# Second attention of a fused two-layer kernel: the reciprocal of a chunk's totals cut in two, its second piece and the scaling of z placed behind maxima of the next group

## The chip, the cores and the metric

The kernel runs on one core of one Trainium2 chip. The metric is the device time of one execution in microseconds (us). The kernel before was run three times: 1402.68, 1404.8 and 1405.77 us, median 1404.8 us. One more execution was taken with the hardware profiler: 1403.8 us, with a span of 1401.9 us from the first instruction to the last.

The engines are named as in the profile: PE (TensorE), PEld (its weight loads), DVE (VectorE), ACT (ScalarE), POOL (GpSimd), SP (SyncE, here only the queue that issues the transfers).

## What is computed

Two layers; each computes x + attention(norm(x)) * silu(ffn(norm(x))). The change is in the attention of the second layer, which is an ordinary causal softmax attention over 2048 tokens with 16 heads of 64, written in the reference for one batch row as

```
q = einsum('bsm,hmd->bshd', x, W_Q) + b_Q        # k and v alike
scores = einsum('bqhd,bkhd->bhqk', q, k) / sqrt(64)
scores = where(causal, scores, -inf)
pattern = softmax(scores, axis=-1)
z = einsum('bhqk,bkhd->bqhd', pattern, v)
attn_out = einsum('bqhd,hdm->bqm', z, W_O) + b_O
```

The softmax is done unnormalized: exp(scores - row maximum), its sum over keys (the totals), and z divided by the totals at the end.

## The kernel before, in words

The second attention (`attention1`) fills the last 850 us of the span. It works on pairs of heads (8 pairs, hp), on chunks of 512 queries (4 per pair, qc) and, in a chunk, on tiles of 128 keys (4, 8, 12 and 16 of them, because of the causal mask). One such key tile is a step s. Four steps make a group k; there are 80 groups, ten to a pair. A chunk ends with group 0, 2, 5 or 9 of its pair; the list `ENDS` holds these group numbers.

All orders are fixed by hand. PE goes through a list of units; each unit writes one of three pairs of PSUM banks in turn (the ring, `RING = 3`), and may do so only when the unit three places earlier has been read by its consumer (`room_for`). The units are:

- "scores": eight matmuls of a step (L1800 three products of split queries and keys, L1803 the subtraction of the row maxima). Consumer: ACT, the exponential into `prob` (L1907).
- "maximum": an unsplit product of queries and keys (L1743, with a mask product L1748 on the diagonal) made only for the row maxima of a later chunk. Consumer: DVE, a maximum over the columns (L1964); after the last one of a row tile's block, a small one over the parts (L1972, neg_max).
- "project", "value", "turn", "mix": projections, values, the turning of the maxima, and z times W_O (L1781), which DVE adds to the output (L2037).

A group has a rows phase, in which maxima and the four scores take turns (`rows_phase`; the table `PLACES` says how many maxima stand ahead of each score, so that five maxima give the order maximum, scores, maximum, scores, ... , maximum), then a whole phase with the other units, and then four times "weigh" (L1822), exp times v of the group's four steps into a bank of its own. If the group before ended a chunk, PE puts "total" (L1769) ahead of the weighing: the sum of the chunk's exponentials, which POOL has added up in `acc` (L1706 the first two steps, L1710 one instruction for each further step; L1678 hides the later keys in diagonal tiles). PE writes the totals into one bank, `side_bank`; DVE takes their reciprocal into `inv` (L1985, 512 columns) and multiplies z by it (L1988, in `scale`), both in one go behind the whole phase. The mix of this chunk waits for the scaled z; it stands one or two groups later.

DVE goes through the same list of units in the same order. Its queue is strict: what is issued behind the reciprocal waits for it, and a ring buffer whose maximum DVE has not read yet holds back the third unit after it on PE.

The reciprocal thus stands at five kinds of places, called here by letter. A: last chunk of the pair before, ahead of a rows phase with five maxima (7 times). B: first chunk, ahead of a rows phase with two maxima, one ahead of the first scores and one ahead of the third (8 times; in the first pair there are six maxima). C: second chunk, five maxima (8 times; eight maxima in the first pair). D: third chunk, five maxima (7 times). E: the third chunk of the last pair, ahead of a rows phase without maxima (once). The last chunk of all has lines of its own (L2020, L2021), which stay.

Of the kernel before, what the change touches and what calls it, by code (L numbers as in the profile page):

```python
# [15 lines left out]
P = 128  # L16
# [3 lines left out]
C = 512  # L20
# [1488 lines left out]
def attention1(nc, a, sh, out):  # L1509

    with ExitStack() as ctx:
        def sb(name, shape, dt=F32):
            return ctx.enter_context(nc.sbuf_tensor(name, shape, dt))

        def sem(name):
            return ctx.enter_context(nc.semaphore(name))
# [14 lines left out]
        ENDS = [s // PER for s in CHUNK_LAST]  # L1531
# [22 lines left out]
        def rows_phase(k):  # L1554

            units = []
            first = TC + sum(MAXIMA[:k])
            for j, count in enumerate(PLACES[MAXIMA[k]]):
                units += TILES[first:first + count]
                first += count  # L1560
                if j < PER:
                    units.append(("scores", k * PER + j, None))
            return units

        def whole_phase(k):

            if k < len(STARTING):
                return STARTING[k]
            return [(kind, k // LAPS + ahead, c) for kind, ahead, c in WHOLE[k % LAPS] if k // LAPS + ahead < NP]
# [29 lines left out]
        inv = sb("inv", [P, C])  # L1599
# [20 lines left out]
        totalled = sem("totalled")  # L1620
        inv_done = sem("inv_done1")
# [8 lines left out]
        side_bank = bank[2 * RING + 1]  # L1630
# [82 lines left out]
        def _(pe):  # L1713
# [44 lines left out]
            def total(g):  # L1758
                if g == FINAL:
                    pe.wait_ge(final_summed, T - 1)  # L1760
                else:
                    pe.wait_ge(summed, CHUNK_LAST[g] + 1)
                if g:

                    pe.wait_ge(inv_done, g)
                else:
                    pe.wait_ge(bias_spread, 1)
                for m in range(2):
                    last = nc.tensor.matmul(side_bank[HALF[m], :], sh.ones[:, 0:W], acc[:, g % 2, m, :],  # L1769
                                            start=True, stop=True)  # L1770
                last.then_inc(totalled, 1)
# [84 lines left out]
            for k in range(GROUPS):  # L1856
# [6 lines left out]
                for s in range(k * PER, (k + 1) * PER):  # L1863
                    weigh(s)
            total(NP * NC - 1)
            for unit in LAST:
                fill(unit)
# [69 lines left out]
        def _(dve):  # L1937
# [9 lines left out]
            def split_low(hp, c):  # L1947
                n = AT["project", hp, c]
                src = unit_both[n % RING]
                at = slice(c * C, (c + 1) * C)  # L1950
                done = nth("project", hp, c) * 2
                dve.wait_ge(act_split, done + 1)
                nc.vector.scalar_tensor_tensor(out=k_lo[hp % 2][:, at], in0=src[:, 0, :], scalar=bias[:, 0, hp:hp + 1],
                                               in1=k_hi[hp % 2][:, at].bitcast(F32), op0=ALU.add, op1=ALU.subtract)
                dve.wait_ge(act_split, done + 2)
                nc.vector.scalar_tensor_tensor(out=q_lo[:, at], in0=src[:, 1, :], scalar=bias[:, 1, hp:hp + 1],
                                               in1=q_hi[:, at].bitcast(F32), op0=ALU.add, op1=ALU.subtract)\
                    .then_inc(unit_freed[n % RING], 1)

            def reduce_tile(hp, i, c):  # L1960
                n = AT["maximum", hp, (i, c)]
                cols = min(C, (i + 1) * P - c * C)
                dve.wait_ge(unit_filled, n + 1)
                nc.vector.tensor_reduce(part_max[:, :, i, c], unit_both[n % RING][:, :, 0:cols], AX_X, ALU.max)\  # L1964
                    .then_inc(unit_freed[n % RING], 1)
                if (i + 1) % TC == 0 and c == i // TC:

                    tiles = [u for u in TILES if u[1] == hp and u[2][0] // TC == c]
                    for r in range(RING):
                        for u in [u for u in tiles if AT[u] % RING == r][-1:]:  # L1970
                            wait_freed(dve, u)
                    nc.vector.tensor_reduce(neg_max[:, c % 2, :, 0:TC], part_max[:, :, c * TC:(c + 1) * TC, 0:c + 1],  # L1972
                                            AX_X, ALU.max, negate=True).then_inc(max_done, 1)

            def spread_maxima(hp, c):
                n = AT["turn", hp, c]
                at = slice(c * C, (c + 1) * C)
                dve.wait_ge(unit_filled, n + 1)
                nc.vector.tensor_tensor(max_rows[:, at].rearrange("r (j c) -> r j c", j=TC),
                                        unit_both[n % RING][:, 0, 0:P].unsqueeze(1).to_broadcast([P, TC, P]),  # L1980
                                        own_tile[:, :, :], ALU.mult).then_inc(unit_freed[n % RING], 1)

            def scale(g):
                dve.wait_ge(totalled, g + 1)
                nc.vector.reciprocal(inv[:, :], side_bank).then_inc(inv_done, 1)  # L1985
                dve.wait_ge(inv_done, g + 1)
                dve.wait_ge(z_copied, g + 1)
                nc.vector.tensor_tensor(z[:, g % 2, :], z[:, g % 2, :], inv[:, :], ALU.mult).then_inc(scaled, 1)  # L1988

            def add_final(s):  # L1990
                kt = s - FINAL_FIRST
                q0 = first_column(NC - 1, kt)
                sums = acc[:, FINAL % 2, :, q0:C]
                if kt == 0:
                    return
                if kt >= (NC - 1) * TC:
                    dve.wait_ge(hidden_later, FINAL * TC + kt - (NC - 1) * TC + 1)
                else:
                    dve.wait_ge(exp_done, s + 1)
                if kt == 1:  # L2000

                    dve.wait_ge(totalled, FINAL - 1)
                    nc.vector.tensor_tensor(sums, prob[:, (s - 1) % PR, :, :], prob[:, s % PR, :, :], ALU.add)\
                        .then_inc(final_summed, 1)
                else:
                    dve.wait_ge(final_summed, kt - 1)
                    nc.vector.tensor_tensor(sums, sums, prob[:, s % PR, :, q0:C], ALU.add).then_inc(final_summed, 1)

            def base_final():
                at = slice(T - TC, T)  # L2010
                dve.wait_ge(unit_freed[AT["mix", NP - 2, NC - 1] % RING], FREED["mix", NP - 2, NC - 1])
                link(nc.vector.tensor_tensor(attn[:, at, :], attn[:, at, :], sh.g[:, at, :], ALU.mult))
                link(nc.vector.tensor_tensor(attn[:, at, :], attn[:, at, :], sh.x[:, at, :], ALU.add))
# [19 lines left out]
            def add_mixed(hp, qc):  # L2033
                n = AT["mix", hp, qc]
                tiles = slice(qc * TC, (qc + 1) * TC)
                dve.wait_ge(unit_filled, n + 1)
                nc.vector.tensor_tensor(attn[:, tiles, :], unit_both[n % RING][:, 0, :].rearrange("p (t d) -> p t d", d=D),  # L2037
                                        attn[:, tiles, :], ALU.add).then_inc(unit_freed[n % RING], 1)
                if hp == NP - 1:

                    wait_freed(dve, ("mix", hp, qc))
                    finish(qc)

            def take(unit):
                kind, hp, what = unit
                if kind == "project":
                    split_low(hp, what)
                elif kind == "maximum":
                    reduce_tile(hp, what[0], what[1])
                elif kind == "turn":  # L2050
                    spread_maxima(hp, what)
                elif kind == "mix":
                    add_mixed(hp, what)
# [9 lines left out]
            nc.vector.tensor_copy(attn[:, :, :], row_o[:, :].unsqueeze(1).to_broadcast([P, T, D])).then_inc(bias_spread, 1)  # L2063
            dve.wait_ge(bias_spread, 1)
            for k in range(GROUPS):
                for unit in rows_phase(k):
                    take(unit)
                for unit in whole_phase(k):
                    take(unit)
                if k - 1 in ENDS:  # L2070
                    scale(ENDS.index(k - 1))
                if k == GROUPS - 1:
                    base_final()
                for s in range(k * PER, (k + 1) * PER):
                    if s >= FINAL_FIRST:
                        add_final(s)
# [98 lines left out]
```

## Time and profile before

| what | value |
|---|---|
| three runs, median | 1404.8 us |
| profiled execution: time, span | 1403.8 us, 1401.9 us |
| PE busy | 1309.4 us (93%) |
| DVE busy | 1012.3 us (72%) |
| ACT busy | 750.4 us (54%) |
| POOL busy | 692.1 us (49%) |
| maxima L1964 on DVE | 320 instructions, 336.8 us |
| reciprocals L1985 on DVE | 31 instructions, 103.9 us |

Busy time is the sum of an engine's instructions. A matmul row of the trace starts when its first product is issued; its end is modelled, so consecutive matmuls overlap in the rows. PEclk is the granted TensorE clock as a share of the full 2.4 GHz.

### The profile page before, as it was taken

How to read it: one execution, taken by the hardware profiler on the slowest of the kernel's cores; microseconds unless marked ns; L12 is line 12 of the kernel's file. 1: busy time of each engine (PE TensorE's matmuls, PEld its weight loads, DVE VectorE, ACT ScalarE, POOL GpSimd, SP SyncE). 2: the span in 40 equal slices, each digit the busy share in tenths (PEclk: the TensorE clock that was granted, in tenths of full speed). 3: DMA queues.
4: the chain of work that ended last, by engine and by line, in shares of the span. 5: the costliest groups of instructions: out<-in, count | busy, mean ns of one | idle time of the engine just before them, and what ended most of it. 6: DMA issues, size and time to landing. Idle time of an engine off the chain costs nothing.

```text
span 1401.9 us, 25496 instructions
## 1 busy us (share of the span) xinstructions
PE 1309.4 (93%) x9902; PEld 672.0 (48%) x9902; DVE 1012.3 (72%) x1497; ACT 750.4 (54%) x1204; POOL 692.1 (49%) x527
## 2 busy tenths in 40 slices
PE   5778999999999987999999999999999999999897
PEld 3653222222222245555555555555555555555554
DVE  7666888888888865766766666766666666766768
ACT  5375777877777774434444344444344344444343
POOL 4401150100101010568777677777677677777671
PEclk9899999999999999999999999999999999999999
DMA  3411410000000000000000000000000000000000
GB/s 107 154 73 57 130 24 1 2 1 2 1 1 1 2 1 1 1 1 1 1 1 1 1 1 1 1 1 1 1 0 1 1 1 1 1 1 1 1 16 16
DMA packets 18165, 21.50 MB, mean 15 GB/s; under 512 B 7784, under 2 KB 15872, under 8 KB 16512
## 3 DMA queue, kind: packets, MB, share of 16 engines
q1 hardware_dynamic: 18048, 19.88, 4.5%
q8 instruction: 81, 1.33, 0.4%
q14 instruction: 36, 0.29, 0.1%
HBM read 14.63 MB, written 5.24 MB: 14 GB/s over the span
## 4 chain that ended last, share of the span: by engine, by line
PE 43%; DVE 11%; ACT 3%; issue 1%; POOL 1%; DVEq 0%; POOLq 0%; ACTq 0%
PE psum L1822 13%; PE psum L1800 12%; DVE part_max L1964 4%; PE psum L1743 4%; DVE inv L1985 4%; PE psum L1803 3%; ACT prob L1907 2%; PE psum L1781 2%; PE psum L1730 2%; PE psum L1769 2%; PE psum L1721 1%; DVE z L1988 1%; PE psum L1723 1%; PE psum L1722 1%; PE psum L1748 1%
## 5 line engine op out<-in xcount | busy, mean ns | idle before, releaser
L1710 POOL TENSOR_TENSOR acc<-acc,prob 128x1024 f32<-128x1024 f32 (+3 forms) x250 | 492.8, 1971 | 87.4 <-ACT prob L1907 57.6
L1907 ACT ACTIVATE prob<-psum 128x1024 f32<-128x1024 f32 (+1 forms) x320 | 283.6, 898 | 352.9 <-PE psum L1803 345.7
L1964 DVE TENSOR_REDUCE part_max<-psum 128x2 f32<-128x1024 f32 (+2 forms) x320 | 336.8, 1064 | 168.8 <-PE psum L1743 84.3
L696 DVE TENSOR_SCALAR w<-psum 128x512 f32<-128x512 f32 x472 | 305.2, 686 | 57.2 <-PE psum L553 43.2
L647 ACT ACTIVATE w<-psum 128x512 f32<-128x512 f32 x552 | 293.7, 600 | 84.5 <-PE psum L553 84.2
L573 PE MATMUL psum<-w,v_cols 128*32 128x512 f32 x2048 | 273.6, 607 | 0.0
L1822 PE MATMUL psum<-prob,v_pair 128*64 128x512 f32 (+3 forms) x1280 | 250.2, 532 | 0.7 <-POOL prob L1678 0.7
L1800 PE MATMUL psum<-q_hi,k_hi 64*128 64x512 f32 (+3 forms) x640 | 138.5, 429 | 31.0 <-DVE part_max L1964 21.2
L1822 PEld LDWEIGHTS psum<-prob,v_pair 128*64 128x64 f32 x1280 | 87.4, 137 | 145.2 <-issue 134.2
L1743 PE MATMUL psum<-k_hi,q_hi 64*128 64x512 f32 (+3 forms) x640 | 131.9, 409 | 6.1 <-DVE part_max L1964 4.5
L1800 PE MATMUL psum<-q_lo,k_hi 64*128 64x512 f32 (+3 forms) x640 | 118.8, 367 | 0.0
L1800 PE MATMUL psum<-q_hi,k_lo 64*128 64x512 f32 (+3 forms) x640 | 118.7, 367 | 0.0
L1803 PE MATMUL psum<-max_rows,ones_r 64*128 64x512 f32 (+3 forms) x640 | 118.6, 366 | 0.0
L1985 DVE RECIPROCAL inv<-psum 128x512 f32<-128x512 f32 x31 | 103.9, 3353 | 16.6 <-PE psum L1769 16.6
L553 PEld LDWEIGHTS psum<-q_rows,k_rows 32*128 32x128 f32 x768 | 40.0, 181 | 153.8 <-ACT w L647 146.3
L397 POOL TENSOR_SCALAR xa<-xa,rstd_j,shift_j 128x128 f32<-128x128 f32 x16 | 7.0, 453 | 208.1 <-DVE shift_j L389 208.1
L1678 POOL TENSOR_SCALAR_AFFINE_SELECT prob<-prob 128x256 f32<-128x256 f32 x128 | 53.5, 425 | 110.9 <-ACT prob L1907 109.9
L553 PE MATMUL psum<-q_rows,k_rows 32*128 32x512 f32 x768 | 101.2, 493 | 0.1
L1800 PEld LDWEIGHTS psum<-q_hi,k_hi 64*128 64x128 f32 x640 | 61.0, 187 | 78.9 <-DVE part_max L1964 48.3
L1743 PEld LDWEIGHTS psum<-k_hi,q_hi 64*128 64x128 f32 x640 | 60.9, 186 | 77.1 <-issue 40.8
L1706 POOL TENSOR_TENSOR acc<-prob 128x1024 f32<-128x1024 f32 x23 | 54.8, 2384 | 42.3 <-ACT prob L1907 40.5
L573 PEld LDWEIGHTS psum<-w,v_cols 128*32 128x32 f32 x2048 | 40.6, 108 | 63.6 <-ACT w L647 53.3
(303 smaller groups left out, 1404.7 us busy)
## 6 DMA issues: line engine op xcount, KB each, us to landing
q_rows<-q_dram SPq DMA_DIRECT2D x12, 256.0 KB
k_rows<-k_dram SPq DMA_DIRECT2D x3, 1024.0 KB
q_dram<-parts SPq DMA_DIRECT2D x2, 1024.0 KB, 4.1
k_dram<-parts SPq DMA_DIRECT2D x2, 1024.0 KB, 6.7
x<-in_L_attn_x SPq DMA_DIRECT2D x4, 256.0 KB, 4.0
mask<-in_L_ffn_attention_mask SPq DMA_DIRECT2D x1, 1024.0 KB, 6.1
x_high<-q_dram SPq DMA_DIRECT2D x4, 256.0 KB
x_low<-k_dram SPq DMA_DIRECT2D x1, 1024.0 KB
```

What stands on the lines that cost most here:

```text
L553: last = nc.tensor.matmul(pair_bank[n % RING][i], k_rows[group][rows, kt * P:(kt + 1) * P], q_rows[group][rows, qc * C:(qc + 1) * C], star ...
L573: last = nc.tensor.matmul(out_bank[turn % 2][h * VW:(h + 1) * VW, :], v_cols[group][:, kt, h, :], w[:, s % WR, h, :], start=(kt == 0), sto ...
L647: nc.scalar.activation(w[:, s % WR, 2 * m + i, :], pair_bank[n % RING][i], ACT.Relu)\
L696: nc.vector.tensor_scalar(w[:, s % WR, 2 * m + 1, :], pair_bank[n % RING][1], 0.0, None, ALU.max)\
L1710: nc.gpsimd.tensor_tensor(sums, sums, prob[:, s % PR, :, q0:C], ALU.add).then_inc(summed, 1)
L1743: last = nc.tensor.matmul(to[:, m, 0:n], q_hi[HALF[m], i * P:(i + 1) * P], k_hi[hp % 2][HALF[m], c * C:c * C + n], start=True, stop=not di ...
L1800: nc.tensor.matmul(to[:, m, q0:C], left[HALF[m], keys], right[HALF[m], at], start=n == 0, stop=False)
L1803: last = nc.tensor.matmul(to[:, m, q0:C], ones_r[HALF[m], :], max_rows[HALF[m], at], start=False, stop=True)
L1822: last = nc.tensor.matmul(out_bank[HALF[m], q0:C], v_pair[hp % 2][:, kt, HALF[m]], prob[:, s % PR, m, q0:C], start=kt == 0, stop=kt == (qc ...
L1907: nc.scalar.activation(prob[:, s % PR, :, q0:C], unit_both[n % RING][:, :, q0:C], ACT.Exp, scale=SCALE)\
L1964: nc.vector.tensor_reduce(part_max[:, :, i, c], unit_both[n % RING][:, :, 0:cols], AX_X, ALU.max)\
L1985: nc.vector.reciprocal(inv[:, :], side_bank).then_inc(inv_done, 1)
```

## The change

The reciprocal is issued as two instructions on columns 0 to 383 and 384 to 511. The first piece stands where the whole one stood. The second piece stands behind the first maximum of the next group's rows phase, and the multiplication of z behind its second maximum; where the rows phase has no maxima, both stand behind it. The semaphore `inv_done` now counts two pieces a chunk, and PE's wait ahead of the next total is doubled with it. PE's, ACT's and POOL's programs keep their order, instruction by instruction.

```
-                    pe.wait_ge(inv_done, g)
+                    pe.wait_ge(inv_done, 2 * g)
...
+            def invert(g, part):
+                at = slice(0, C - P) if part == 0 else slice(C - P, C)
+                if part == 0:
+                    dve.wait_ge(totalled, g + 1)
+                nc.vector.reciprocal(inv[:, at], side_bank[:, at]).then_inc(inv_done, 1)
+
             def scale(g):
-                dve.wait_ge(totalled, g + 1)
-                nc.vector.reciprocal(inv[:, :], side_bank).then_inc(inv_done, 1)
-                dve.wait_ge(inv_done, g + 1)
+                dve.wait_ge(inv_done, 2 * (g + 1))
                 dve.wait_ge(z_copied, g + 1)
                 nc.vector.tensor_tensor(z[:, g % 2, :], z[:, g % 2, :], inv[:, :], ALU.mult).then_inc(scaled, 1)
+
+            def end_scale(g, left):
+                if left == 2:
+                    invert(g, 1)
+                else:
+                    scale(g)
+
+            def take_rows(k):
+                g = ENDS.index(k - 2) if k - 2 in ENDS else None
+                left = 2 if g is not None else 0
+                for unit in rows_phase(k):
+                    take(unit)
+                    if unit[0] == "maximum" and left:
+                        end_scale(g, left)
+                        left -= 1
+                while left:
+                    end_scale(g, left)
+                    left -= 1
...
             for k in range(GROUPS):
-                for unit in rows_phase(k):
-                    take(unit)
+                take_rows(k)
                 for unit in whole_phase(k):
                     take(unit)
                 if k - 1 in ENDS:
-                    scale(ENDS.index(k - 1))
+                    invert(ENDS.index(k - 1), 0)
```

DVE at place A, before: the reciprocal, z, and then the five maxima (L1964; part_max) of the next group, with the small maximum over the parts (L1972) behind the first.

```order
L1964 TENSOR_REDUCE part_max<-psum 128x2 x3
L1985 RECIPROCAL inv<-psum 128x512
L1988 TENSOR_TENSOR z<-z,inv 128x512
L1964 TENSOR_REDUCE part_max<-psum 128x2
L1972 TENSOR_REDUCE neg_max<-part_max 128x2x4
L1964 TENSOR_REDUCE part_max<-psum 128x2 x4
L2037 TENSOR_TENSOR xa<-psum,xa 128x4x128
```

The same place after the change (the lines below the edit have moved in the file: L1987 is the reciprocal, L1992 the scaling).

```order
L1987 RECIPROCAL inv<-psum 128x384
L1964 TENSOR_REDUCE part_max<-psum 128x2
L1972 TENSOR_REDUCE neg_max<-part_max 128x2x4
L1987 RECIPROCAL inv<-psum 128x128
L1964 TENSOR_REDUCE part_max<-psum 128x2
L1992 TENSOR_TENSOR z<-z,inv 128x512
L1964 TENSOR_REDUCE part_max<-psum 128x2 x3
L2060 TENSOR_TENSOR xa<-psum,xa 128x4x128
```

The second piece now stands ahead of the second maximum and z ahead of the third.

DVE at place B, which follows: two maxima, and then the addition of the mix (L2037 before, L2060 after), whose product on PE reads the scaled z of this very chunk. First before, then after.

```order
L1985 RECIPROCAL inv<-psum 128x512
L1988 TENSOR_TENSOR z<-z,inv 128x512
L1964 TENSOR_REDUCE part_max<-psum 128x2 x2
L2037 TENSOR_TENSOR xa<-psum,xa 128x4x128
L1979 TENSOR_TENSOR max_rows<-psum,own_tile 128x512
```

```order
L1987 RECIPROCAL inv<-psum 128x384
L1964 TENSOR_REDUCE part_max<-psum 128x2
L1987 RECIPROCAL inv<-psum 128x128
L1964 TENSOR_REDUCE part_max<-psum 128x2
L1992 TENSOR_TENSOR z<-z,inv 128x512
L2060 TENSOR_TENSOR xa<-psum,xa 128x4x128
L1979 TENSOR_TENSOR max_rows<-psum,own_tile 128x512
```

Between z and the mix that needs it there were two maxima; now there is nothing.

## Rows read from the trace of the kernel before

**Rows 1.** Waits of PE: us in total, times, longest.
```profile
PE psum L1800 <- DVE part_max L1964: 21.2, 25, 1.9
```

**Rows 2.** The scaling by its line (ns min/median/max); the 256-column reciprocals by form.
```profile
L1988 DVE TENSOR_TENSOR z<-z,inv x31: 691/693/1392, 579.4 to 1368.9; 128x512 f32<-128x512 f32 x31
```
```profile
L2020 DVE RECIPROCAL inv<-psum 128x256 f32<-128x256 f32 x2 | 3.5, 1756 | 1.2 <-PE psum L1769 1.2
```

**Rows 3.** Timeline, place A: start us, us, engine, line, names [idle before].
```profile
1200.52 3.36 DVE L1985 RECIPROCAL inv<-psum 128x512 f32<-128x512 f32 x1 [1.41 <-PE psum L1769]
1202.39 2.16 POOL L1710 TENSOR_TENSOR acc<-acc,prob 128x512 f32<-128x512 f32 x2
...
1202.89 0.29 PE L1748 MATMUL psum<-causal,ident_b 64*128 64x128 bf16 x4
...
1203.91 1.18 DVE L1988 TENSOR_TENSOR z<-z,inv 128x512 f32<-128x512 f32 x1
...
1206.28 0.50 PE L1800 MATMUL psum<-q_hi,k_hi 64*128 64x512 f32 x2 [1.88 <-DVE part_max L1964]
1206.37 0.18 DVE L1972 TENSOR_REDUCE neg_max<-part_max 128x8 f32<-128x24 f32 x1
...
1208.62 2.39 POOL L1706 TENSOR_TENSOR acc<-prob 128x1024 f32<-128x1024 f32 x1 [4.08 <-ACT prob L1907]
...
1209.03 0.49 PE L1800 MATMUL psum<-q_hi,k_hi 64*128 64x512 f32 x2
```

**Rows 4.** Timeline, place B.
```profile
1217.59 1.22 DVE L1964 TENSOR_REDUCE part_max<-psum 128x2 f32<-128x1024 f32 x1
...
1219.41 1.23 DVE L1964 TENSOR_REDUCE part_max<-psum 128x2 f32<-128x1024 f32 x1 [0.60 <-PE psum L1743]
...
1220.75 1.16 PE L1781 MATMUL psum<-wo,z 128*128 128x128 f32 x8
1220.90 0.82 POOL L1678 TENSOR_SCALAR_AFFINE_SELECT prob<-prob 128x256 f32<-128x256 f32 x2 [0.32 <-ACT prob L1907]
```

**Rows 5.** Timeline, place C.
```profile
1236.52 0.28 PE L1748 MATMUL psum<-causal,ident_b 64*128 64x128 bf16 x4
...
1238.93 4.94 POOL L1710 TENSOR_TENSOR acc<-acc,prob 128x1024 f32<-128x1024 f32 x2 [2.95 <-ACT prob L1907]
...
1238.94 0.50 PE L1800 MATMUL psum<-q_hi,k_hi 64*128 64x512 f32 x2 [0.92 <-DVE part_max L1964]
...
1241.70 0.50 PE L1800 MATMUL psum<-q_hi,k_hi 64*128 64x512 f32 x2
```

**Rows 6.** Timeline, place D.
```profile
1268.91 0.28 PE L1748 MATMUL psum<-causal,ident_b 64*128 64x128 bf16 x4
...
1269.49 0.69 DVE L1964 TENSOR_REDUCE part_max<-psum 128x2 f32<-128x512 f32 x1
...
1271.32 4.89 POOL L1710 TENSOR_TENSOR acc<-acc,prob 128x1024 f32<-128x1024 f32 x2 [3.85 <-ACT prob L1907]
...
1271.91 0.96 DVE L1964 TENSOR_REDUCE part_max<-psum 128x2 f32<-128x768 f32 x1 [0.23 <-PE psum L1748]
...
1273.01 0.42 PE L1800 MATMUL psum<-q_hi,k_hi 64*128 64x512 f32 x2
```

**Rows 7.** Timelines of DVE and POOL around another product of two SBUF tiles.
```profile
1327.68 1.92 DVE L1943 TENSOR_TENSOR xa<-xa,g 128x512 f32<-128x512 f32 x1
```
```profile
1326.70 7.13 POOL L1710 TENSOR_TENSOR acc<-acc,prob 128x1024 f32<-128x1024 f32 x4
```

**Rows 8.** Windows: us, busy of PE, PEld, DVE, ACT, POOL, then PEclk, DMA.
```profile
1206.28:1210.48 4.20, 4.18 (x34) 2.70 (x34) 3.76 (x4) 2.27 (x3) 1.86 (x1) 1.00 0.00 0
...
1310.16:1315.43 5.27, 5.27 (x35) 3.80 (x35) 3.76 (x4) 2.17 (x3) 2.65 (x2) 0.68 0.00 0
```

**Rows 9.** Timelines of DVE and PE, place E.
```profile
1370.79 2.56 DVE L2007 TENSOR_TENSOR acc<-acc,prob 128x1024 f32<-128x1024 f32 x2
```
```profile
1372.70 1.16 PE L1781 MATMUL psum<-wo,z 128*128 128x128 f32 x8
```

## The prediction

> **What bounds the kernel now.** I read the page first (PE is busy almost throughout the second attention), then the waits of PE, then the timeline of PE, DVE, ACT and POOL around each of the 31 reciprocals. The waits say how little there is to win: PE's matmul stream stands still for DVE's maxima 21.2 us in all, in 25 pieces [rows 1]. The timeline says where. At place A the scores behind the second maximum wait 1.88 us, since DVE reads the first maximum only after the reciprocal and z [rows 3]. At C there is a like wait of 0.92 us in the same position [rows 5]. At B and D PE does not wait. The reader should see that PE carries the time: whatever delays a unit on PE, at any of these places, is added to the end, as PE has no slack to give it back; and that DVE is nearly full in exactly these rows phases, where a maximum of 1024 columns takes 1.22 us [rows 4].
>
> **The change part by part.** Only DVE's order changes. The work is the same: a reciprocal of 512 columns takes 3.36 us [rows 3], so 384 columns take 2.52 and 128 take 0.84 (an estimate by columns). The 256-column ones took 1756 ns, against 1676 for half of the large one [rows 2, 3]: a fixed cost of 0 to 0.08 us for the extra instruction, at most 2.5 us over 31; I take 0 and leave the rest to the range. What counts is when each ring buffer is freed, and when z comes. I replay the four places with the trace's own durations: DVE starts on a product 0.04 us after PE's row ends (my choice, from the spacing of such pairs), its next instruction starts 0.08 before the last ends (L1972 ends at 1206.55 and the maxima behind it begin at 1206.46 in the timeline), PE follows a freed buffer by 0.05.
>
> *Place A* [rows 3]. The first piece ends at 1200.52 + 2.52 = 1203.04. The first maximum's product is there at 1202.89 + 0.29 = 1203.18. DVE reads it 1203.22 to 1204.44; the second scores start at 1204.49 and not at 1206.28. That is the gain, 1.8 us at this point. But now come the small maximum (to 1204.76), the second piece (1204.68 to 1205.52), the second maximum (1205.44 to 1206.66), z (1206.58 to 1207.27 if nothing disturbs it) and the third maximum (to 1208.41). The fourth scores need the third maximum's buffer: 1208.46, against 1209.03 before. Of 1.8 us 0.5 stay, since DVE has the same work to do ahead of the third maximum as before. Seven places: -3.5 us.
>
> *Place B* [rows 4]. No wait to remove: DVE read its first maximum at 1217.59, and PE did not wait. Now the second piece goes between the maxima (there is room: 1218.81 + 0.84 = 1219.65 at the latest, against a start at 1219.41), and z goes behind the second, 1220.58 to 1221.27. POOL is idle till 1220.90, so z should have its way. But the mix at 1220.75 multiplies this z. It now starts at 1221.32: +0.57 us, and what is queued behind it on PE (the turn, the weighing) waits along. Eight places: +4.6 us.
>
> *Places C and D: z meets POOL.* z has both its inputs in SBUF. Alone it takes 691 ns [rows 2]; at A it took 1.18 us: it started at 1203.91 while POOL's additions ran to 1204.55, and ended 0.54 after these [rows 3]. The product of L1943, two SBUF inputs as well, started at 1327.68 and took 1.92 us; POOL's first addition of that row started at 1326.70 and lasts about 2.39 [rows 3, 7], to 1329.09; the product ended 0.51 later. So such a product waits for the end of POOL's current instruction and then takes about 0.55 us; it gets in between two of POOL's instructions. Maxima and reciprocals, which read PSUM, show nothing of it.
> The Trainium skill (SBUF — State Buffer, section Who interferes with whom) says that a VectorE instruction with two SBUF inputs and a GpSimd one that reads SBUF exclude each other, and that the first to issue keeps the port for its whole instruction. The 1.18 us alone would also fit a mere slowing by 1.7, which would make C and D cheaper (a rival below); the 1.92 us fits only the exclusion, so the trace agrees with the page.
>
> At C [rows 5] I work back from the second scores at 1238.94: ahead of them a short maximum (0.96, as in rows 6), z (0.69) and the reciprocal (3.36), which thus began near 1233.95; its first piece is over at 1236.47, before the first maximum's product (1236.80). Maximum to 1237.79, second piece to 1238.55, second maximum 1238.47 to 1239.70. z is up at 1239.62, but POOL's addition started at 1238.93 and lasts to 1241.32: z ends at 1241.87. Before, z ran ahead of the group's first exponential, when POOL had nothing. Third maximum 1241.79 to 1243.02, fourth scores at 1243.07 against 1241.70: +1.37 us, and the 0.92 us won at the second scores is in that already. Without POOL z would end at 1240.31, and the fourth scores would start 0.1 us before or after where they did. Eight places: +11.0 us.
>
> At D [rows 6] the product is there at 1269.19; first maximum (0.69) to 1269.92, second piece to 1270.68, second maximum 1270.60 to 1271.83, z up at 1271.75, POOL busy since 1271.32 and to 1273.71: z ends at 1274.26. Third maximum (0.96) to 1275.14, fourth scores at 1275.19 against 1273.01: +2.18 us. Without POOL it would be about +0.6, since here no wait is removed and two instructions are put in front of the third maximum. Seven places: +15.3 us.
>
> *Place E* [rows 9]. Both late pieces stand behind the final chunk's additions, which ended at 1373.35 and would now end 0.84 + 0.69 earlier, so z ends at about 1373.3; the mix at 1372.70 waits 0.6 us for it. +0.6 us.
>
> *The clock.* At A the stall of 1.9 us was followed in four of the seven places by a stretch at the lower level, 1.2 GHz: the row from 1310.16 (the last of the four) shows a mean of 0.68 and 5.27 us for the units that took 4.20 at 1.00 [rows 8]. Each cost 1.07 us. Bounds: all four go (-4.3 us), or the new waits at C and D, up to 2.2 us in one piece, bring the same number again, or one at each of 15 places (+16, less the 4.3). I take 0, since the stalls of the length that had it at A now stand at D.
>
> The sum: -3.5 + 4.6 + 11.0 + 15.3 + 0.6 = +28.0 us. On the profiled execution's own 1403.8 us that is 1431.8; the median of the runs lies 1.0 above it, so 1432.8, and I say 1433.
>
> **The rivals.**
> - *z loses the race at A.* POOL's first addition starts 2.34 us after the second scores (1206.28 to 1208.62 [rows 3]), which gives 1206.83 in the new order; z is up at 1206.58. The margin is 0.25 us. If POOL is first, z ends at 1209.77 and the fourth scores start near 1210.96, 1.9 later than before and not 0.5 earlier: 2.4 x 7 = 17 us more, 1450. For it speaks the small margin, against it that the arithmetic puts z first.
> - *POOL does not matter.* z takes 0.69 us wherever it stands. A -3.5, B +4.6, C 8 x 0.1, D 7 x 0.6, E +0.6: +6.7, and with the stalls shorter the clock's 4.3 us come back: about 1407. Rows 7 speak against it.
> - *z is only slowed*, by 1.7, as the 1.18 us could be read: z 0.5 us longer at C and D, 15 places, +7.5 on +6.7, clock unchanged: 1419.
> - *Faster.* The freed buffers carry through: the 1.88 us at 7 places A and 0.92 at 8 places C go, with four slow stretches of 1.07, and nothing comes back: -13.2 - 7.4 - 4.3 = -25, 1380. It decides on DVE's room between the second and the third maximum: it needs 1.5 us of idle time there (0.84 for the second piece, 0.69 for z). Ahead of the third maximum at D DVE was idle for 0.23 us [rows 6], and at A it had a backlog. For it speaks only that PE's named waits do stand where the edit works.
> - *The edit does little*: gains at A and losses at B cancel, C and D are absorbed by units that wait on ACT. 1405. For it speaks that ACT's exponentials also hold PE back in these phases; against it that the delays at C and D are longer than an exponential.
>
> **How the numbers follow.** Forecast 68%; race lost at A 12%; POOL of no matter 7%; slowed only 6%; faster 5%; little 2%. What this kernel's measurement can tell from no change is about 0.2%, 2.8 us. Slower: 68 + 12 + 6 and most of the 7, 90%; within: 2 + 2, 4%; faster: 5 + 1, 6%. The range runs from 1417, which takes in the slowed-only case, to 1450, the lost race; the forecast's own terms (fixed cost up to +2.5, clock from -4.3 to some +8) lie within.
>
> **What would show it.** At A the second scores start about 1.8 us earlier after the weighing than before, and a new wait of about 1 us stands at the third scores; z before POOL's L1706. At B the mix waits for z (L1992) in PE's waits, about 0.6 us, eight times. At C and D z takes 2.2 to 2.5 us instead of 0.69, and the fourth scores wait for a maximum. The total of z's line grows by about 25 us (15 places by 1.6 to 1.8), and that of the reciprocal stays. DVE busy grows with it, though nothing was added. Wrong would be the forecast if z showed 0.69 us at C and D, or if the third maxima began as early as before.

## The result and the profile after

The changed kernel takes 1447.9 us (median of four runs, 1439.6 to 1450.0); the kernel before, run beside it, 1405.0. The ratio is 1.030, 95% interval 1.028 to 1.032: slower, by 43 us. The forecast was 1433 with a range from 1417 to 1450, so direction and range held, and 15 of the 43 us were not in the sum. The profiled execution took 1449.97 us.

Page of the changed kernel: busy time, share and instructions by engine.

```profile
PE 1333.8 (92%) x9902; PEld 685.7 (47%) x9902; DVE 1026.7 (71%) x1528; ACT 751.1 (52%) x1204; POOL 699.3 (48%) x527
```

DVE is busy 14.4 us longer, although the change adds only 31 short instructions. Its reciprocals and z by form (busy us, mean ns, idle before), and z by its line (min/median/max in ns):

```profile
L1987 DVE RECIPROCAL inv<-psum 128x384 f32<-128x384 f32 x31 | 79.2, 2553 | 16.6 <-PE psum L1769 16.6
L1987 DVE RECIPROCAL inv<-psum 128x128 f32<-128x128 f32 x31 | 29.4, 948 | 0.0
L1992 DVE TENSOR_TENSOR z<-z,inv 128x512 f32<-128x512 f32 x31 | 45.3, 1462 | 0.0
```

```profile
L1992 DVE TENSOR_TENSOR z<-z,inv x31: 674/693/2472, 585.9 to 1418.2; 128x512 f32<-128x512 f32 x31
```

The whole reciprocal took 3353 ns in the mean, so the cut costs 2553 + 948 - 3353 = 148 ns each time, 4.6 us of DVE work in all. The 31 z took 45.3 us together, and in the kernel before

```profile
L1988 DVE TENSOR_TENSOR z<-z,inv 128x512 f32<-128x512 f32 x31 | 25.5, 823 | 1.1
```

That is 19.8 us more; the longest z is now 2472 ns [rows 2 had 1392]. The busy time of DVE grows by less than these two together, since it counts only once the time in which the rows of two instructions overlap, and more of them now follow each other directly. The waits of PE in the second attention, against [rows 1]:

```profile
PE psum L1800 <- DVE part_max L1964: 39.1, 49, 1.8
...
PE psum L1781 <- DVE z L1992: 4.5, 8, 0.7
```

The scores now wait for the maxima 49 times instead of 25, and for 39.1 us instead of 21.2. The eight waits of the mix for z are seven of the places B (0.52 to 0.54 us) and place E (0.74 us).

**Place A**, timeline of the group that answers to [rows 3]:

```profile
1243.92 0.95 DVE L1987 RECIPROCAL inv<-psum 128x128 f32<-128x128 f32 x1
...
1245.87 0.68 DVE L1992 TENSOR_TENSOR z<-z,inv 128x512 f32<-128x512 f32 x1
1246.01 0.50 PE L1800 MATMUL psum<-q_hi,k_hi 64*128 64x512 f32 x2 [0.83 <-DVE part_max L1964]
1246.08 2.71 POOL L1706 TENSOR_TENSOR acc<-prob 128x1024 f32<-128x1024 f32 x1 [2.31 <-ACT prob L1907]
...
1247.73 0.50 PE L1800 MATMUL psum<-q_hi,k_hi 64*128 64x512 f32 x2 [0.29 <-DVE part_max L1964]
```

z is 0.21 us ahead of POOL and short; it is POOL's instruction that is held up (2.71 us instead of 2.39). The stall of 1.88 us is gone, but 0.83 and 0.29 us stand at the third and fourth scores.

**Place B**, answering to [rows 4]:

```profile
1259.20 0.68 DVE L1992 TENSOR_TENSOR z<-z,inv 128x512 f32<-128x512 f32 x1
...
1260.02 1.13 PE L1781 MATMUL psum<-wo,z 128*128 128x128 f32 x8 [0.54 <-DVE z L1992]
```

The mix waits for z, at seven of the eight places B. In the first pair, with six maxima, it doesn't; there the later scores wait 0.65 and 0.49 us for maxima, and the place costs 0.71 us.

**Places C and D**, answering to [rows 5, 6], first C:

```profile
1277.85 1.16 DVE L1964 TENSOR_REDUCE part_max<-psum 128x2 f32<-128x1024 f32 x1
...
1278.19 7.64 POOL L1710 TENSOR_TENSOR acc<-acc,prob 128x1024 f32<-128x1024 f32 x3 [3.12 <-ACT prob L1907]
...
1278.92 2.19 DVE L1992 TENSOR_TENSOR z<-z,inv 128x512 f32<-128x512 f32 x1
...
1281.04 2.35 DVE L1964 TENSOR_REDUCE part_max<-psum 128x2 f32<-128x1024 f32 x2
1282.31 0.50 PE L1800 MATMUL psum<-q_hi,k_hi 64*128 64x512 f32 x2 [1.80 <-DVE part_max L1964]
```

```profile
1313.40 7.64 POOL L1710 TENSOR_TENSOR acc<-acc,prob 128x1024 f32<-128x1024 f32 x3 [3.82 <-ACT prob L1907]
...
1313.86 2.47 DVE L1992 TENSOR_TENSOR z<-z,inv 128x512 f32<-128x512 f32 x1
...
1317.25 0.80 PE L1800 MATMUL psum<-q_hi,k_hi 64*128 64x512 f32 x2 [1.82 <-DVE part_max L1964]
```

POOL's first addition takes 2.38 us of the row. At C it ends at 1280.57, and z 0.54 us later; at D, with the same length, at 1315.78, and z 0.55 us later. Only then come the third maximum and the fourth scores. (At C another 0.40 us stands at the third scores.) The matmul rows of D from the stall on last 0.80 and 0.63 us instead of 0.50 and 0.40: the lower clock. The windows from the end of one weighing to the start of the next show it for a whole place. First the kernel before, C and D; then after: C, D, and D in another pair, where the clock stayed up (columns as in rows 8).

```profile
1236.30:1244.80 8.50, 7.58 (x57) 4.84 (x57) 7.55 (x8) 4.10 (x4) 5.58 (x3) 1.00 0.00 0
1268.75:1275.81 7.06, 7.06 (x64) 4.89 (x64) 5.90 (x7) 4.11 (x4) 4.34 (x2) 1.00 0.00 0
```

```profile
1275.55:1286.92 11.37, 9.17 (x59) 5.78 (x57) 8.89 (x9) 4.11 (x4) 8.30 (x4) 0.85 0.00 0
1310.82:1321.35 10.53, 8.65 (x64) 5.93 (x63) 8.25 (x7) 4.10 (x4) 7.52 (x4) 0.84 0.00 0
...
758.18:767.31 9.13, 7.25 (x65) 4.97 (x64) 8.11 (x7) 4.11 (x4) 6.26 (x3) 1.00 0.00 0
```

D costs 9.13 - 7.06 = 2.07 us at full clock and 3.47 with a stretch at 1.2 GHz. C costs 2.87; I put about 1.5 of it down to the clock, an estimate, since the fourth scores came 1.36 us later than before ahead of the stretch, and no C but the last (+1.55 to the next weighing) was without one. Such stretches stood in the kernel before at 4 of 7 places A and nowhere else in these phases; after, at none of A, at 7 of 8 places C and 6 of 7 places D.

Place by place, from the end of one weighing to the end of the next, the two profiled executions differ by:

| | by place | sum | of it the clock |
|---|---|---|---|
| A (7) | -0.57, where the clock had been low -1.7 to -1.95 | -8.95 | -5 |
| B (8) | +0.57, first one +0.71 | +4.75 | 0 |
| C (8) | +2.4 to +3.8; last one +1.6 | +23.97 | +13 |
| D (7) | +2.07 once, else +3.5 to +3.6 | +23.29 | +9 |
| E (1) | the mix waits 0.74 | +0.77 | 0 |

The sum is 43.8 us: the clock's net part is about 17 and the places' own about 27. The clock's part is an estimate for C, as said. The two spans differ by 46.3 us: another 2.9 us arise ahead of the first weighing, where the programs are the same (the profile of the changed kernel has a stretch at the lower clock there, at 559 us, and that of the kernel before has none), and -0.45 us at one group of the last pair.

### The profile page after: what moved, and what is told of

The parts are those of the page before. It is cut to its first block, busy times and chain, and to the rows that moved or that the text cites. A ratio compares the mean times of both kernels' runs of the same rounds, so it can differ in the third digit from the quotient of the medians.

```text
span 1448.2 us, 25527 instructions
## 1 busy us (share of the span) xinstructions
PE 1333.8 (92%) x9902; PEld 685.7 (47%) x9902; DVE 1026.7 (71%) x1528; ACT 751.1 (52%) x1204; POOL 699.3 (48%) x527
## 4 chain that ended last, share of the span: by engine, by line
PE 41%; DVE 14%; ACT 2%; issue 2%; POOL 1%; DVEq 0%; POOLq 0%; ACTq 0%
PE psum L1822 16%; DVE part_max L1964 9%; PE psum L1800 8%; PE psum L1743 3%; DVE z L1992 3%; PE psum L1781 2%; PE psum L1803 2%; PE psum L1769 2%; PE psum L1730 2%; ACT prob L1907 2%; PE psum L1721 1%; PE psum L1722 1%; PE psum L1723 1%; PE psum L1748 1%; DVE inv L1987 1%
## 5 line engine op out<-in xcount | busy, mean ns | idle before, releaser
L1964 DVE TENSOR_REDUCE part_max<-psum 128x2 f32<-128x1024 f32 (+2 forms) x320 | 334.1, 1058 | 191.4 <-PE psum L1748 108.8
L1800 PE MATMUL psum<-q_hi,k_hi 64*128 64x512 f32 (+3 forms) x640 | 140.4, 435 | 49.8 <-DVE part_max L1964 39.1
L1987 DVE RECIPROCAL inv<-psum 128x384 f32<-128x384 f32 (+1 forms) x62 | 108.5, 1751 | 16.6 <-PE psum L1769 16.6
L1706 POOL TENSOR_TENSOR acc<-prob 128x1024 f32<-128x1024 f32 x23 | 57.1, 2481 | 31.1 <-ACT prob L1907 29.5
```

What stands on the lines that cost most here:

```text
L1800: nc.tensor.matmul(to[:, m, q0:C], left[HALF[m], keys], right[HALF[m], at], start=n == 0, stop=False)
L1987: nc.vector.reciprocal(inv[:, at], side_bank[:, at]).then_inc(inv_done, 1)
```

## The experiments

Each was compared with the kernel before on the same chip (median 1404.4 to 1405.1 us there).

### The cut alone

```
-                take_rows(k)
+                for unit in rows_phase(k):
+                    take(unit)
                 for unit in whole_phase(k):
                     take(unit)
                 if k - 1 in ENDS:
                     invert(ENDS.index(k - 1), 0)
+                    invert(ENDS.index(k - 1), 1)
+                    scale(ENDS.index(k - 1))
```

> The changed kernel with both pieces of the reciprocal and then z at the place where the whole reciprocal stood; nothing is behind a maximum. It measures the cut alone. Theory (z behind the second maximum waits for POOL's running instruction, because both its inputs lie in SBUF; new stalls of 2 us bring half-clock stretches): the two pieces took 2.56 + 0.95 us against 3.36, so 0.15 us more at A and C, 15 places, about 2 us, and z is at 0.69 us at B, C and D again: 1405 to 1409. Rival (the cut itself costs, by the extra instructions, and the order little): most of the 43 us stay, 1435 or more.

Measured: 1405.5 us, ratio 1.000 (0.999 to 1.001). The cut costs nothing that can be measured in the time; the 43 us come from the order.

### z alone moved

The kernel before, the reciprocal whole:

```
+                    passed += unit[0] == "maximum"
+                    if passed == 2 and late is not None:
+                        scale(late)          # the product alone
+                        late = None
...
                 if k - 1 in ENDS:
-                    scale(ENDS.index(k - 1))
+                    invert(ENDS.index(k - 1))
```

> The kernel before, reciprocal whole and in its old place, z alone moved behind the second maximum (behind the rows phase where there is none). Theory: at C z is up after POOL's start and waits to its end, the fourth scores 1.4 us late; at D the second maximum ends at about 1271.7 and POOL starts at 1271.3, so again 2.2 us late; A gains about 0.7, B loses about 0.5 (the mix waits for z); with the half-clock stretches of the changed kernel: 1435 to 1450, about as the changed kernel. Rival (the second piece behind the first maximum is what costs): within 5 us of 1405.

Measured: 1439.7 us, ratio 1.024 (1.023 to 1.026). Moving z alone brings 35 of the 43 us. z took 2.67 us at C (2.31 at the first) and 2.65 at D, and 12 of these 15 places had a stretch at the lower clock. The second piece behind the first maximum is not the cause; with it come the remaining 8 us. At A z alone gains more, 0.87 us a place instead of 0.57.

### The order kept, the reciprocal in PSUM

```
-                    pe.wait_ge(inv_done, 2 * g)
+                    pe.wait_ge(scaled, g)
...
-                nc.vector.reciprocal(inv[:, at], side_bank[:, at]).then_inc(inv_done, 1)
+                nc.vector.reciprocal(side_bank[:, at], side_bank[:, at]).then_inc(inv_done, 1)
...
-                nc.vector.tensor_tensor(z[:, g % 2, :], z[:, g % 2, :], inv[:, :], ALU.mult).then_inc(scaled, 1)
+                nc.vector.tensor_tensor(z[:, g % 2, :], z[:, g % 2, :], side_bank, ALU.mult).then_inc(scaled, 1)
```

> The changed kernel, order and cut unchanged, but the reciprocal is written back into the PSUM bank of the totals and z is multiplied from there, so that z's product has one SBUF input and one PSUM input; PE's wait ahead of the next total is on the scaled z. Theory: z takes about 0.7 us at every place, also beside POOL; A 7 x -0.6, B 8 x +0.6, C about 0, D 7 x +0.6 (two instructions ahead of the third maximum), E +0.6, and the half-clock stretches mostly go: 1403 to 1413. Rival 1 (not POOL, but the mere place of z between second and third maximum delays the scores): 1440 or more, with z short in the trace. Rival 2 (POOL and DVE collide over something other than the second SBUF input, for instance the write of z into SBUF): z stays at 2.2 and 2.5 us at C and D and the time at 1440 or more.

Measured: 1401.9 us, ratio 0.9975 (0.996 to 0.999). The same order of the same instructions is 46 us faster, by the place of one operand. z by its line, and z at C beside POOL's additions:

```profile
L1992 DVE TENSOR_TENSOR z<-z,psum x31: 669/673/689, 583.4 to 1369.3; 128x512 f32<-128x512 f32 x31
```

```profile
1237.91 0.67 DVE L1992 TENSOR_TENSOR z<-z,psum 128x512 f32<-128x512 f32 x1
```

```profile
1237.18 4.92 POOL L1710 TENSOR_TENSOR acc<-acc,prob 128x1024 f32<-128x1024 f32 x2 [3.12 <-ACT prob L1907]
```

z starts 0.73 us into POOL's instruction, as in the changed kernel, and takes 0.67 us. So the second SBUF input is what collided, and not the write of z. The collision is gone for POOL too: its first addition at A, which z had stretched to 2.71 us, is at 2.38 to 2.39 again at all seven places, beside a z that starts as far ahead of it. By place: A -9.0 us in all (clock included), B +4.7, C -0.8, D +1.8, E +0.8; no stretch at the lower clock at any of these places. Both rivals fall.

### z directly behind the second piece

```
                     if unit[0] == "maximum" and left:
-                        end_scale(g, left)
-                        left -= 1
+                        end_scale(g, 2)
+                        end_scale(g, 1)
+                        left = 0
```

> The changed kernel with z directly behind the second piece, both behind the first maximum. Theory: at C z is up at about 1238.65 on the old kernel's time scale and POOL starts at 1238.93, at D 0.5 us ahead of POOL, so z comes first at both and takes 0.69 us: A -0.6, B +0.6, C about 0, D +0.5 us each; 1403 to 1413 with few half-clock stretches. Rival (work between the maxima is what costs, whatever POOL does): the same instructions stand between first and third maximum, so 1440 or more.

Measured: 1418.8 us, ratio 1.009 (1.007 to 1.011). The theory held for z, which came first and took 0.69 us at C and D (the first pair's C excepted: 2.82), and for the clock (one stretch, at that C); the time is 6 us above my window. The misses are at A (-0.17 a place where the clock had been high, -0.6 expected: the third scores wait 1.61 us there), B (+0.86, 0.6), C (+0.27, 0) and D (+0.97, 0.5), and 4.2 in the first C. Timeline of PE at D, third and fourth scores:

```profile
1288.34 0.50 PE L1800 MATMUL psum<-q_hi,k_hi 64*128 64x512 f32 x2 [0.84 <-DVE part_max L1964]
...
1289.61 0.39 PE L1800 MATMUL psum<-q_hi,k_hi 64*128 64x512 f32 x2
```

I had priced the delay of the third maximum only. But with 1.6 us of work between the first and the second maximum it is the third scores that wait, and PE still has these and the next maximum to do (1.27 us) before the fourth. So here it is better to put work ahead of a later maximum than of an earlier one, if z does not collide there: at A, where z waits for POOL in neither order, the changed kernel gains 0.57 us and this one 0.17.

### The stall without POOL

The order of the changed kernel with the reciprocal in PSUM, and ahead of z at C, D and E:

```
+                if g % NC in (1, 2):
+                    nc.vector.reciprocal(inv[:, 0:2 * P], side_bank[:, 0:2 * P])
```

> The changed order with the reciprocal in PSUM (1401.9 us) and, ahead of z at C, D and E, one reciprocal of 256 columns of that bank into a tile nobody reads (about 1.7 us; the result does not change). It puts back on DVE the time for which z waited at C and D (1.5 and 1.8 us), with nothing that POOL could hold up. Theory (the loss is DVE's delay of the third maximum, from whatever cause, and a stall of this length on PE brings the half-clock stretch by itself): 15 x 1.6 + 1.7 = 26 us, and 8 to 14 half-clock stretches of 1.0 to 1.5 us: 1436 to 1450, granted clock 0.97. Rival (the lower clock has to do with the collision of DVE and POOL, or with the run, and not with PE's stall): 1424 to 1430, clock 0.985.

Measured: 1445.3 us, ratio 1.028 (1.026 to 1.030), granted clock 0.974. DVE and PE at C:

```profile
1268.13 1.74 DVE L1993 RECIPROCAL inv<-psum 128x256 f32<-128x256 f32 x1
1269.78 0.63 DVE L1994 TENSOR_TENSOR z<-z,psum 128x512 f32<-128x512 f32 x1
```

```profile
1271.60 0.50 PE L1800 MATMUL psum<-q_hi,k_hi 64*128 64x512 f32 x2 [1.89 <-DVE part_max L1964]
...
1273.37 0.79 PE L1721 MATMUL psum<-x_high,w_high 128*128 128x512 f32 x1
```

Here nothing collides, PE stalls 1.89 us (2.76 at the first C), and the lower clock follows (0.79 us for a matmul of 0.50), at all eight places C. At D the stall came out shorter, 1.64 us, and the stretch followed at two of seven; at E PE stalls 2.40 us for z, and one follows. Time and clock lie in the theory's window. So the collision is not needed for the clock's loss: a stall of PE at this place, made by DVE alone, brings it.

### The change at A alone

```
+                if g is not None and g % NC != NC - 1:
+                    g = None
...
                     invert(ENDS.index(k - 1), 0)
+                    if ENDS.index(k - 1) % NC != NC - 1:
+                        invert(ENDS.index(k - 1), 1)
+                        scale(ENDS.index(k - 1))
```

> The change kept at A alone, both inputs of z in SBUF as before; at B, C, D and E both pieces and z at the old place. Theory: A gave -0.57 us a place in the changed kernel and -1.7 to -1.95 where the kernel before had a half-clock stretch, -8.9 us in all; nothing else moves: 1394 to 1399, with no half-clock stretch at A. Rival (the clock's loss is a matter of chance, not of the stall of 1.9 us): stretches at A as often as before, 1401.

Measured: 1396.6 us, ratio 0.995 (0.993 to 0.996), no stretch at the lower clock at A. The sum of A from weighing to weighing is -8.95 us, the same as in the changed kernel, 5 us of it the clock's. The change is a gain at the one place it fits.

### The kernel before with the reciprocal in PSUM

The edit is that of the PSUM experiment above, on `scale` of the kernel before.

> The kernel before in its own order, reciprocal whole, but written back into the PSUM bank of the totals and read from there for z. Only A had z beside POOL (1.17 us). Theory: z 0.67 us at A too, the first maximum 0.5 us earlier, PE's stall at A 1.4 us instead of 1.88; 7 x -0.5 and perhaps the four half-clock stretches (-4.3): 1397 to 1402. Rival (z's width at A is a matter of its place, not of its operands): within 1.5 us of 1405.

Measured: 1397.0 us, ratio 0.995 (0.994 to 0.996), z 0.69 us at all 31 places. At A -0.47 to -0.49 us, -1.6 to -1.85 where the clock had been low. So PE's stall of 1.4 us that is left there was not followed by the lower clock at any of the seven places, where the one of 1.88 us was at four. A was not the only place with z beside POOL, as I had written: at the last C z had taken 1.39 us [the longest of rows 2] and ended 0.55 us behind POOL's addition, and this place gains 0.73 us.

### Late z, and late piece

The two experiments together point to a better order: keep everything out from between the maxima, and put z where it is not waited for. B, D and E, where there was nothing to win, keep the old order. First with the whole reciprocal (in PSUM):

```
+            BEHIND = {1: 9, 3: 4}     # C: behind the rows phase; A: behind the fourth maximum
...
+                if late is not None and late % NC not in BEHIND:
+                    late = None
...
+                    passed += unit[0] == "maximum"
+                    if late is not None and passed == BEHIND[late % NC]:
+                        scale(late)
```

> Reciprocal whole at its old place, result in PSUM; z at C behind the whole rows phase, at A behind the fourth maximum, at B, D and E at its old place. Nothing is put between the maxima whose buffers the scores need. Theory: A: first maximum 1203.9 on the old time scale, second to 1206.5, third to 1207.6, fourth scores at 1207.7 instead of 1209.0, -1.4 us each and the four half-clock stretches gone; C: first maximum at 1237.2, fourth scores at 1240.7 instead of 1241.7, -1.0 each: 1405 - 9.8 - 4.3 - 8 = 1383, 1380 to 1390. Rival (PE's own work or ACT's exponentials bound these phases as soon as DVE is out of the way): half of that or less, 1394 or more.

Measured: 1384.8 us, ratio 0.986 (0.985 to 0.988): A -1.26 a place, or -2.4 to -2.65 with the clock, C -0.8. PE's wait on the maxima is down from 21.2 us to

```profile
PE psum L1800 <- DVE part_max L1964: 6.4, 20, 0.6
```

The same with the reciprocal in two pieces, the second one directly ahead of the late z (edit: `behind = {1: 9, 3: 4}.get(g % NC)` in `take_rows`):

> As the kernel with late z, and the reciprocal in two pieces of which at A and C the second goes late too, directly ahead of z. Theory: the first maxima start when their products are there, another 0.6 us earlier at A and 0.4 at C, but only a part of it reaches the fourth scores; at A the second piece and z (1.6 us) come close to the mix that needs z. 1376 to 1386, 0 to 7 us below the kernel with late z alone. Rival (at A the mix now waits for z): equal or slower than that one, with a wait of PE's L1781 on z.

Measured: 1386.3 us, ratio 0.987 (0.986 to 0.988); not told apart from the one before. That is just above my window, and the rival came true. C gained 0.95 us a place instead of 0.8, but A only 1.0 instead of 1.26, since the mix there waits for z:

```profile
PE psum L1781 <- DVE z L1992: 3.7, 7, 0.5
```

And the late z with the reciprocal in SBUF:

> The fastest order (whole reciprocal in place, z at A behind the fourth maximum, at C behind the rows phase), but with the reciprocal in SBUF as in the kernel before, so that z has two SBUF inputs. Theory: at A z is up while POOL adds, waits 1 to 2 us and the mix waits for it; at C it waits up to 2.4 us ahead of the splits of keys and queries: 1390 to 1405 instead of 1384.8. Rival (late in the phase z's wait is covered, only the order matters): 1383 to 1388.

Measured: 1388.5 us, ratio 0.988 (0.987 to 0.990), below my window and half a microsecond above the rival's. z collides at A (1.20 to 1.24 us) and in the first C (2.88). At A, where POOL's L1706 runs from 1095.00 to 1097.38:

```profile
1096.69 1.24 DVE L1990 TENSOR_TENSOR z<-z,inv 128x512 f32<-128x512 f32 x1
```

This costs 0.28 us a place at A. At the other seven places C z took 0.68 to 0.69 us, although POOL was adding there as well: z came up just as one addition ended and began 0.10 to 0.16 us ahead of the next, which then took 2.8 us instead of 2.4. DVE and POOL at the second C (POOL's first addition ends at 722.06, the next begins at 722.21):

```profile
722.09 0.68 DVE L1990 TENSOR_TENSOR z<-z,inv 128x512 f32<-128x512 f32 x1
```

```profile
719.67 7.85 POOL L1710 TENSOR_TENSOR acc<-acc,prob 128x1024 f32<-128x1024 f32 x3
```

In the first C z came 0.02 us too late. So at C this order went well by luck in timing, and not because POOL was idle. Even the lost race added nothing by the next weighing there, which speaks for the rival (z's wait is covered so late in the phase), but it is one place. The order brings most of the gain. The operand's part is about 2.2 us, the sum over the places in the two profiled executions; the rest of the 3.7 us between the medians is not shown to be its doing.

## Why the prediction was right, and where it was short

**Place A** held: forecast -0.5, measured -0.57 us, which is what the replay itself gave (1209.03 - 1208.46) before it was rounded for the sum. z won the race by 0.21 us (0.25 expected), so the first rival did not occur. The sign named for z's line, about 25 us more, came out as 19.8: it left out the 0.5 us by which z gets shorter at each A.

**Place B** held: +0.57 forecast, +0.57 measured at seven places, the mix waiting for z. The first pair's B has other waits and +0.71.

**C and D** held, to a hundredth, in what the order does up to the fourth scores. From the end of the weighing to the fourth scores, C grew from 5.40 to 6.76 us, +1.36 (forecast +1.37), and D from 4.26 to 6.43, +2.17 (forecast +2.18). At the next weighing of D +2.07 are left. That the agreement is so close owes something to the collision: both pieces of the reciprocal were longer than assumed (0.14 us together), but z's end hangs on the end of POOL's addition and not on its own start. The experiment with PSUM shows that the wait for POOL is the cause. "POOL does not matter" and "z is only slowed" fall with it: z ended 0.54 us behind POOL's instruction every time, whatever was left of that instruction. The PSUM run, 1401.9, is also near the 1407 that I gave for POOL of no matter (C and D came out at -0.1 and +0.25 us a place, where that rival had +0.1 and +0.6). The chances had a slip there: 1407 would have been within 2.8 us of no change, and most of its 7% was counted as slower.

**The fixed cost** of the second piece was 0.15 us, outside my bound of 0.08. The step was wrong, not the rows: half of the large reciprocal contains half of its fixed cost, so comparing it with a 256-column one shows only half of what a cut costs. Two of 1756 ns against one of 3353 give 0.16 us. It did not show in the time.

**The clock** is the term that was mis-sized. "I take 0, since the stalls of the length that had it at A now stand at D" was to be four stretches of 1.07 us as before. They were 13 of 1.0 to 2.4 us, about +22 against -5 for the four that went, net about +17. That lies above even the stated upper bound (one at each of 15 places, +16 less 4.3, so +11.7), because the stretches were dearer: 1.7 us each in the mean, and from weighing to weighing even those at A had cost 1.1 to 1.4 us, not 1.07. The choice of 0 was wrong for two reasons that the rows already showed. First, C had to be counted beside D. The 0.92 us won at the second scores is waited out at the later ones, on top of the new 1.37: 0.40 us at the third scores and 1.80 at the fourth, which made 15 places and not 7. Second, with four in seven at 1.88 us, 15 such stalls make eight or nine stretches, not four. The run without POOL shows that such a stall brings them without a collision. The total stayed within the range because the rest of the sum was right (27 us measured, 28 forecast) and the range was wide upward for another reason, the race at A: that part is luck.

**Faster** needed 1.5 us of room on DVE between the second and third maximum. There was none: at A 1.8 us won at the second scores came down to 0.57.

## What to carry to other kernels

An operation that is cheap where it stands can be dear a microsecond later, because of what the other engines do at that time: before moving a product of two SBUF tiles, look at what POOL runs at the new place, and if it must stand there, leave one operand in PSUM. Where an engine is full between two hand-overs, cutting its work up only moves the wait from the first hand-over to the next; move work to behind the last one that somebody waits for. And where such stalls were followed by a lower clock before, a stall on TensorE in an otherwise dense stream is priced with its own length plus the chance of a stretch at 1.2 GHz behind it, counted for every place that has a stall of that length.

## What the runs showed of the hardware that I had not expected

- A DVE product of two SBUF tiles and POOL's additions hold each other up, in both directions: where POOL's instruction was first, z ended 0.54 to 0.55 us after it, whatever was left of it to wait out (0.5 to 2.3 us in these runs), and it got in between two additions that follow each other by 0.14 us. Where z was first, POOL's L1706 grew by 0.32 us. With one operand in PSUM z took 669 to 689 ns at all 31 places, also 0.7 us into POOL's instruction. The Trainium skill (SBUF — State Buffer, section Who interferes with whom) says that a DVE instruction with at most one SBUF input, outside the modes that use two ports, does not contend with GpSimd; these rows agree.
- Whether a stretch at 1.2 GHz follows goes with the length of PE's stall, but not by a fixed limit in these runs. Counted over the places A to D of all twelve profiled executions: 0 of 11 stalls of 1.3 to 1.4 us, 2 of 15 of 1.6 us, 27 of 35 of 1.8 to 1.9 us (4 of 7 in the kernel before), 15 of 18 of 2.0 to 2.9 us were followed by one. Length alone does not decide: PE's wait for L1979 ahead of the last C, 2.0 to 2.8 us, was followed by one in 6 of the 12 and by none in the other 6, among them both kernels compared here. What decides stays open. The time of the changed kernel varies with the clock: its fastest run, 1439.6 us, had a granted clock of 0.977, the other three 0.968 to 0.970.
- The reciprocal on DVE goes by 6.3 ns a column plus 0.15 us: 948 ns for 128 columns, 1756 for 256, 2553 for 384, 3353 for 512.
